# Leaky step of the two graph layers split between ScalarE and VectorE, and a new order of the work, in a four-layer graph kernel

## The chip, the cores and the metric

The kernel runs on one core of a Trainium2 chip. The metric is device time in microseconds for one execution over the whole batch; lower is better. The kernel before was run three times: 1826.78, 1825.92 and 1824.29 us, median 1825.92 us.

## What is computed

Four attention layers follow each other on 128 graphs of 128 nodes with 256 features, float32. Layers 0 and 2 are eight-head attention weighted by an adjacency matrix; layers 1 and 3 are single-head graph attention with a leaky step. The reference, cut:

```python
# layer 0 (_L0_gnn_ref): heads of 32, adj as a log weight, then out projection and layer norm
logits = jnp.einsum('bhqd,bhkd->bhqk', q, k) / np.sqrt(DK)
logits = logits + jnp.log(jnp.clip(adj, ADJ_MIN, None))[:, None, :, :]
attn = jax.nn.softmax(logits, axis=-1)
...
# layers 1 and 3 (_L1_gnn_ref, _L3_gnn_ref)
feat_proj = jnp.einsum('bnh,oh->bno', feats, fc_w) + fc_b
logits = q + jnp.swapaxes(k, 2, 1)                     # q, k: one column each from feat_proj
masked = logits + (1.0 - adj_mat) * NEG_INF
masked = jnp.where(masked >= 0, masked, LEAKY_SLOPE * masked)   # slope 0.01
atten = jax.nn.softmax(masked, axis=-1)
out = jnp.einsum('bnm,bmh->bnh', atten, feat_proj) + feats
...
# layer 2 (_L2_gnn_ref): heads of 32, a per-node bias pair, adj as a log weight, residual
```

## The kernel before, in words

The batch is cut into 64 groups of two graphs (GROUP = 2). The kernel is a software pipeline over turns: in turn t, each engine walks its own list in the table ORDER, and an entry (lag, name, where, n) means "do this step for group t - lag". So one turn does each step once, but for groups of different age: layer 0 for group t, layer 1 for t - 1, layer 2 for t - 2, layer 3 for t - 3 and so on. There are five lists, one for each engine, written out by hand; within an engine, nothing overtakes. The engines meet through semaphores only. Before the full turns the pipeline fills, after them it drains.

The steps the texts below speak of, by engine, with the lines of the profile:

- TensorE, the three-pass products (L877, L878, L879, function three_pass): each float32 product is made of three passes over split operands. q, k, v0 (layer 0) and q2, k2 take 12 matmuls each; each half of v2 (128x258), fc (128x258) and out_proj takes 6.
- TensorE, scores: 16 matmuls with 32-row weights (L942), once as "scores" and once, with sides exchanged, as "again"; between the two VectorE finds the row maximum. "A" is layer 0, "B" layer 2. B also adds column terms (L951), and "shift" (L965) subtracts the maximum. These go to banks 0 to 3 of PSUM.
- TensorE, sums: den (L986) and use (L977), 16 matmuls each with 32-column weights; wide (L992) spreads the inverse denominators.
- TensorE, transposes: turn_x (L1053), turn_max (L1047), turn_rows (L1098), mask (L1081, spreads the k column of a graph layer), turn_p (L1087, the softmaxed matrix). mix (L1093) is the last product of a graph layer.
- VectorE: max (L768) reads the four score banks in four reductions, all of which wait for the one semaphore of the last scores matmul; weigh (L792); den (L799, L801, L803); mask (L732 twice, then the leaky step L736 and its row minimum L739); inv (L855).
- ScalarE: soft (L547 and L551, exponentials of the scores), exp (L629) and inv (L636) of the graph layers, copies out of PSUM (among them turn_p, L641).

The leaky step works on negated logits, so that it is a minimum: min(x, 0.01 x). Before the change it is one VectorE instruction on a 128x256 tile in SBUF:

```python
dve.scalar_tensor_tensor(logits[layer][:, :, :], logits[layer][:, :, :], SLOPE,
                         logits[layer][:, :, :], ALU.mult, ALU.min).then_inc(leaked[layer], 1)
```

Steps other than scores take the banks 4 to 7 of PSUM in rotation, in the order of TensorE's list (BANK); wait_drained makes TensorE wait until the last user of a bank has been read (last_reader). FILLERS puts a few spare matmuls (L1031) ahead of some steps of the first groups.

## Time and profile before

| | |
|---|---|
| median of three runs | 1825.92 us |
| the profiled execution | 1827.11 us, span of the instructions 1825.2 us |
| PE busy | 1786.8 us (98% of the span) |
| DVE busy | 1496.7 us (82%) |
| ACT busy | 1345.0 us (74%) |
| POOL busy | 562.3 us (31%) |
| mean granted TensorE clock | 0.989 |

PE is TensorE's matmul row, PEld its weight loads, DVE VectorE, ACT ScalarE, POOL GpSimd. In the timeline a row gives the start, the duration and the instruction. Matmuls are pipelined, so their durations overlap; what a step takes of TensorE's time is the distance from its start to the start of the next step. A wait in brackets names what ended the engine's idle time.

### The profile page before, as it was taken

How to read it: one execution, taken by the hardware profiler on the slowest of the kernel's cores; microseconds unless marked ns; L12 is line 12 of the kernel's file. 1: busy time of each engine (PE TensorE's matmuls, PEld its weight loads, DVE VectorE, ACT ScalarE, POOL GpSimd, SP SyncE). 2: the span in 40 equal slices, each digit the busy share in tenths (PEclk: the TensorE clock that was granted, in tenths of full speed). 3: DMA queues.
4: the chain of work that ended last, by engine and by line, in shares of the span. 5: the costliest groups of instructions: out<-in, count | busy, mean ns of one | idle time of the engine just before them, and what ended most of it. 6: DMA issues, size and time to landing. Idle time of an engine off the chain costs nothing.

```text
span 1825.2 us, 69034 instructions
## 1 busy us (share of the span) xinstructions
PE 1786.8 (98%) x28449; PEld 1676.6 (92%) x28449; DVE 1496.7 (82%) x3359; ACT 1345.0 (74%) x3664; POOL 562.3 (31%) x667
## 2 busy tenths in 40 slices
PE   6999999999999999999999999999999999999996
PEld 6899999999999999999999999999999999999985
DVE  4678888888888888888888888888888888888885
ACT  3577787787787787787787787787787787787774
POOL 2232332332332332332332332332332332332321
PEclk7999999999999999999999999999999999999998
DMA  3111111111111111111111111111111111111100
GB/s 110 34 31 40 46 36 40 46 37 40 46 37 40 46 37 40 46 36 40 46 37 40 46 37 40 46 37 40 46 37 40 46 37 40 45 37 40 40 14 18
DMA packets 48260, 74.57 MB, mean 41 GB/s; under 512 B 5456, under 2 KB 21968, under 8 KB 47952
## 3 DMA queue, kind: packets, MB, share of 16 engines
q1 hardware_dynamic: 47376, 69.49, 12.1%
q8 instruction: 230, 3.77, 0.9%
q10 hardware_dynamic: 576, 0.68, 0.1%
q14 instruction: 78, 0.64, 0.1%
HBM read 53.37 MB, written 16.78 MB: 38 GB/s over the span
## 4 chain that ended last, share of the span: by engine, by line
PE 95%; DVE 3%; ACT 1%; issue 1%; POOL 0%; DVEq 0%; POOLq 0%; ACTq 0%
PE banks L877 17%; PE banks L942 15%; PE banks L879 15%; PE banks L878 15%; PE banks L986 7%; PE banks L1093 7%; PE banks L977 6%; PE banks L965 3%; PE banks L992 3%; PE banks L1081 2%; PE banks L1087 1%; PE banks L1053 1%; PE banks L1047 1%; PE banks L951 1%; PE banks L1031 0%
## 5 line engine op out<-in xcount | busy, mean ns | idle before, releaser
L478 POOL TENSOR_TENSOR weights_B<-weights_B,adj 128x512 f32<-128x512 f32 x64 | 82.4, 1288 | 815.9 <-ACT weights_B L551 815.9
L792 DVE TENSOR_TENSOR weights_A<-banks,adj 128x512 f32<-128x512 f32 x192 | 131.1, 684 | 77.2 <-ACT banks L547 77.1
L456 POOL TENSOR_TENSOR xt_lo<-x_t,xt_hi 128x512 fp32r<-128x512 f32 x64 | 82.1, 1282 | 335.6 <-ACT xt_hi L580 335.6
L877 PE MATMUL banks<-w_hi_f,xt_hi 128*128 128x258 f32 x512 | 164.6, 321 | 0.6 <-DVE xt_lo L656 0.6
L768 DVE TENSOR_REDUCE least_B<-banks 128x4 f32<-128x512 f32 x256 | 162.8, 678 | 0.0
L877 PE MATMUL banks<-w_hi_v,xt_hi 128*128 128x258 f32 (+1 forms) x512 | 152.2, 297 | 10.5 <-DVE w_lo_v L656 9.8
L768 DVE TENSOR_REDUCE least_cols_A<-banks 128x4 f32<-128x512 f32 x256 | 158.4, 681 | 4.5 <-PE banks L942 4.5
L636 ACT ACTIVATE logits<-logits,f_inv 128x128 f32<-128x128 f32 x256 | 90.9, 415 | 86.8 <-DVE f_inv L855 86.7
L877 PE MATMUL banks<-xt_hi,w_hi_q 128*128 128x256 f32 x512 | 150.5, 294 | 0.0
L879 PE MATMUL banks<-w_lo_v,xt_hi 128*128 128x258 f32 (+1 forms) x512 | 146.5, 286 | 0.0
L878 PE MATMUL banks<-w_hi_f,xt_lo 128*128 128x258 f32 x512 | 145.8, 285 | 0.0
L551 ACT ACTIVATE banks<-banks,v_B 128x256 f32<-128x256 f32 x384 | 145.5, 470 | 0.0
L878 PE MATMUL banks<-w_hi_v,xt_lo 128*128 128x258 f32 (+1 forms) x512 | 145.2, 284 | 0.0
L879 PE MATMUL banks<-xt_lo,w_hi_q 128*128 128x256 f32 x512 | 145.1, 283 | 0.0
L879 PE MATMUL banks<-w_lo_f,xt_hi 128*128 128x258 f32 x512 | 144.8, 283 | 0.0
L879 PE MATMUL banks<-xt_lo,w_hi_k 128*128 128x256 f32 x512 | 144.1, 281 | 0.0
L877 PE MATMUL banks<-xt_hi,w_hi_k 128*128 128x256 f32 x512 | 143.9, 281 | 0.0
L878 PE MATMUL banks<-xt_hi,w_lo_k 128*128 128x256 f32 x512 | 143.8, 281 | 0.0
L1093 PE MATMUL banks<-fpt,fp 128*128 128x128 f32 x1024 | 142.5, 282 | 1.3 <-DVE sum_t L816 0.7
L878 PE MATMUL banks<-xt_hi,w_lo_q 128*128 128x256 f32 x512 | 143.4, 280 | 0.0
L1093 PEld LDWEIGHTS banks<-fpt,fp 128*128 128x128 f32 x1024 | 125.2, 192 | 10.4 <-DVE sum_t L816 1.0
L792 DVE TENSOR_TENSOR weights_B<-banks,adj 128x512 f32<-128x512 f32 x192 | 128.2, 673 | 4.8 <-ACT banks L551 4.8
(185 smaller groups left out, 6068.5 us busy)
## 6 DMA issues: line engine op xcount, KB each, us to landing
x_t<-x_t_dram SPq DMA_DIRECT2D x64, 256.0 KB, 2.7
x_in<-x_dram SPq DMA_DIRECT2D x64, 256.0 KB, 2.6
out_dram<-x_out SPq DMA_DIRECT2D x64, 256.0 KB, 2.0
adj_t<-adj_t_dram SPq DMA_DIRECT2D x64, 128.0 KB, 2.1
adj<-adj_dram SPq DMA_DIRECT2D x64, 128.0 KB, 2.6
scratch<-weights_dram SPq DMA_DIRECT2D x9, 256.0 KB, 6.6
scratch<-weights_dram ACTq DMA_DIRECT2D x2, 256.0 KB, 4.8
out_bias<-L_gnn_bo_dram ACTq DMA_DIRECT2D x1, 128.0 KB, 7.5
```

Source lines behind the costliest of these rows:

```text
L478: pool.tensor_tensor(units, units, weight_of[where][:, G.four, :, :].unsqueeze(2).broadcast_to([P, GROUP, 2, P]), ALU.mult).then_inc(first ...
L551: last = act.activation(to[:, cols(g, 2 * P)], x[:, cols(g, 2 * P)], ACT.Exp, bias=v["B"][:, G.odd, g, DIM + 1:WIDE], scale=-1.0)
L636: last = act.activation(logits[where][:, g, :], logits[where][:, g, :], ACT.Copy, scale=f_inv[where][:, g:g + 1])
L768: dve.tensor_reduce(to, bank[SCORE_BANKS[n]].rearrange("p (u m) -> p u m", u=UNITS), axis=AX.X, op=ALU.min).then_inc(maxed[where], 1)
L792: dve.tensor_tensor(weights[where][:, n, :].rearrange(units, g=GROUP, h=2), bank[SCORE_BANKS[n]].rearrange(units, g=GROUP, h=2), weight_of ...
L877: pe.matmul(out_ap, left_hi(k), right_hi(k), start=(k == 0), stop=False)
L878: pe.matmul(out_ap, left_lo(k), right_hi(k), start=False, stop=False)
L879: last = pe.matmul(out_ap, left_hi(k), right_lo(k), start=False, stop=(k == KT - 1))
L942: last = pe.matmul(bank[SCORE_BANKS[r]][:, cols(u)], left[row_group(r), G.odd, half, cols(g)], right[row_group(r), G.odd, half, cols(g)], ...
L977: last = pe.matmul(to[row_group(r), cols(u)], v[s][:, G.odd, g, head:head + HEAD_DIM], weights[s][:, r, cols(u)], start=True, stop=True)
L986: last = pe.matmul(to[row_group(r), 0:P], sums[:, u, :], weights[s][:, r, cols(u)], start=(u == 0), stop=(u == UNITS - 1), skip_group_chec ...
L1093: last = pe.matmul(to[:, cols(k * GROUP + g)], fp[layer][:, g, cols(k)], fpt[layer][:, g, :], start=True, stop=True)
```

## The change

Two things are changed. First, the leaky step is split: ScalarE writes the copy scaled by 0.01 into the PSUM bank that the mask transposes had filled (it has been read by then), raises the new semaphore sloped, and VectorE takes the minimum of that copy and the logits. TensorE may use that bank again only when the minimum is done (leaked instead of masked). "leak" becomes a step of its own on both engines. Second, all five lists of ORDER are written anew; of these the diff below shows a line of each side.

```diff
--- before.py
+++ after.py
@@ -25,37 +25,38 @@
 ORDER = {
     "tensor": [
-        (0, "again", "A", 0), (0, "shift", "A", 0), (1, "fc", "1", 0), (2, "turn_rows", "2", 0), (3, "wide", "B", 0),
...
+        (0, "shift", "A", 0), (3, "wide", "B", 0), (1, "fc", "1", 0), (1, "fc", "1", 1), (2, "q", "2", 0),
...
@@ -266,6 +267,7 @@
         fp_ready = {n: sem(f"fp_ready_{n}") for n in "13"}
         qk_ready = {n: sem(f"qk_ready_{n}") for n in "13"}
         masked = {n: sem(f"masked_{n}") for n in "13"}
+        sloped = {n: sem(f"sloped_{n}") for n in "13"}
         leaked = {n: sem(f"leaked_{n}") for n in "13"}
         f_maxed = {n: sem(f"f_maxed_{n}") for n in "13"}
         f_exped = {n: sem(f"f_exped_{n}") for n in "13"}
@@ -344,7 +346,7 @@
             if name == "out_proj":
                 return summed, GROUP * g + n + 1
             if name == "mask":
-                return masked[where], GROUP * (g + 1)
+                return leaked[where], g + 1
             if name == "mix":
                 return (x2_ready if where == "1" else out_ready), g + 1
             return {"turn_x": x_biased.get(where), "turn_p": fpt_ready.get(where),
@@ -623,6 +625,11 @@
                     elif name == "fc":
                         act.wait_ge(filled[b], turn.after(G, *key))
                         act.activation(fp[where][:, n, :], bank[b][:, 0:WIDE], ACT.Copy).then_inc(fp_ready[where], 1)
+                    elif name == "leak":
+                        act.wait_ge(masked[where], GROUP * (G.no + 1))
+                        act.activation(bank[BANK["mask", where, 0]][:, 0:GROUP * P],
+                                       logits[where][:, :, :].rearrange("p g m -> p (g m)"), ACT.Copy, scale=SLOPE
+                                       ).then_inc(sloped[where], 1)
                     elif name == "exp":
                         act.wait_ge(f_maxed[where], G.no + 1)
                         for g in range(GROUP):
@@ -732,9 +739,14 @@
                     dve.scalar_tensor_tensor(logits[layer][:, g, :], bank[b][:, cols(g)],
                                              fp[layer][:, g, DIM:DIM + 1], penalty[:, G.four, g, :],
                                              ALU.add, ALU.add).then_inc(masked[layer], 1)
+
+            def leak(layer, G):
+
+                flat = logits[layer][:, :, :].rearrange("p g m -> p (g m)")
                 dve.wait_ge(masked[layer], GROUP * (G.no + 1))
-                dve.scalar_tensor_tensor(logits[layer][:, :, :], logits[layer][:, :, :], SLOPE,
-                                         logits[layer][:, :, :], ALU.mult, ALU.min).then_inc(leaked[layer], 1)
+                dve.wait_ge(sloped[layer], G.no + 1)
+                dve.tensor_tensor(flat, bank[BANK["mask", layer, 0]][:, 0:GROUP * P], flat, ALU.min
+                                  ).then_inc(leaked[layer], 1)
                 dve.wait_ge(leaked[layer], G.no + 1)
                 dve.tensor_reduce(f_neg_max[layer][:, :], logits[layer][:, :, :], axis=AX.X, op=ALU.min
                                   ).then_inc(f_maxed[layer], 1)
@@ -861,6 +873,8 @@
                                           ).then_inc(qk_ready[where], 1)
                     elif name == "mask":
                         mask(where, G, turn)
+                    elif name == "leak":
+                        leak(where, G)
                     elif name == "mix":
                         residual(where, G, turn)
 
```

Where the lists move work, in full turns:

TensorE, layer 0, from the scores of the next group to its maximum transposed (kt_A, qt_A: scores; least_cols_A: turn_max). Before:

```order
L1081 MATMUL banks<-ident,fp 128x128 x2
L942 MATMUL banks<-kt_A,qt_A 128x128 x16
L877 MATMUL banks<-w_hi_v,xt_hi 128x258
L878 MATMUL banks<-w_hi_v,xt_lo 128x258
L879 MATMUL banks<-w_lo_v,xt_hi 128x258
L877 MATMUL banks<-w_hi_v,xt_hi 128x258
L878 MATMUL banks<-w_hi_v,xt_lo 128x258
L879 MATMUL banks<-w_lo_v,xt_hi 128x258
L1053 MATMUL banks<-ident,x 128x128 x4
L986 MATMUL banks<-weights_B,sums 32x128 x16
L977 MATMUL banks<-weights_B,v_B 32x128 x16
L1047 MATMUL banks<-ident,least_cols_A 128x128
```

After:

```order
L893 MATMUL banks<-xt_lo,w_hi_k 128x256
L956 MATMUL banks<-kt_A,qt_A 128x128 x16
L991 MATMUL banks<-weights_B,v_B 32x128 x16
L1000 MATMUL banks<-weights_B,sums 32x128 x16
L1112 MATMUL banks<-ident,c_cols 128x128
L1067 MATMUL banks<-ident,x 128x128 x4
L1061 MATMUL banks<-ident,least_cols_A 128x128
L956 MATMUL banks<-qt_A,kt_A 128x128 x16
L979 MATMUL banks<-least_rows_A,minus_pick 128x128 x16
```

Behind the scores stood one half of v2, the x transposes, den B and use B; now use B, den B, turn_rows and the x transposes stand there, the half of v2 has gone ahead of mask 3, and the second scores pass and its shift follow.

TensorE, layer 2, from its scores on (kt_B, qt_B: scores). Before:

```order
L986 MATMUL banks<-weights_A,sums 32x128 x16
L977 MATMUL banks<-weights_A,v_A 32x128 x16
L942 MATMUL banks<-kt_B,qt_B 128x128 x16
L951 MATMUL banks<-c_rows,minus_pick 128x256 x8
L1093 MATMUL banks<-fpt,fp 128x128 x4
L877 MATMUL banks<-xt_hi,w_hi_q 128x256
```

After:

```order
L956 MATMUL banks<-kt_B,qt_B 128x128 x16
L965 MATMUL banks<-c_rows,minus_pick 128x256 x8
L1000 MATMUL banks<-weights_A,sums 32x128 x16
L991 MATMUL banks<-weights_A,v_A 32x128 x16
L1101 MATMUL banks<-ident,logits 128x128 x2
L891 MATMUL banks<-xt_hi,w_hi_q 128x256
```

Where mix 3 (fpt, fp) followed the column terms (c_rows), den A and use A now follow them, and the transposes of layer 1's matrix (logits) come next.

VectorE, layer 1, around the mask (fp, penalty). Before:

```order
L792 TENSOR_TENSOR weights_A<-banks,adj 128x512
L816 TENSOR_TENSOR sum_t<-banks,sum_t 128x512
L860 TENSOR_TENSOR fp<-fp,cols_tile 128x2x2
L792 TENSOR_TENSOR weights_A<-banks,adj 128x512
L732 SCALAR_TENSOR_TENSOR logits<-banks,fp,penalty 128x128 x2
L736 SCALAR_TENSOR_TENSOR logits<-logits 128x256
L739 TENSOR_REDUCE f_neg_max<-logits 128x2
L799 RECIPROCAL banks<-banks 128x128
L801 CAST inv_hi_A<-banks 128x128
L803 SCALAR_TENSOR_TENSOR inv_parts_A<-banks,low_row,inv_hi_A 128x128
L656 TENSOR_TENSOR xt_lo<-sum_t,xt_hi 128x512
```

After:

```order
L804 TENSOR_TENSOR weights_A<-banks,adj 128x512
L872 TENSOR_TENSOR fp<-fp,cols_tile 128x2x2
L804 TENSOR_TENSOR weights_A<-banks,adj 128x512
L739 SCALAR_TENSOR_TENSOR logits<-banks,fp,penalty 128x128 x2
L804 TENSOR_TENSOR weights_A<-banks,adj 128x512
L748 TENSOR_TENSOR logits<-banks,logits 128x256
L751 TENSOR_REDUCE f_neg_max<-logits 128x2
L797 TENSOR_SCALAR adj<-adj_t 128x256
L780 TENSOR_REDUCE least_B<-banks 128x4
L867 RECIPROCAL f_inv<-f_den 128x2
L780 TENSOR_REDUCE least_B<-banks 128x4
```

The mask and the leaky step were neighbours; now the third weighting of A lies between them, and a copy of adj and the first maximum of B between the row minimum and the reciprocal f_inv.

## Rows read from the trace of the kernel before

**Rows 1.** Windows view, full turns: busy us of each engine, then granted clock

```profile
800.00:1200.00 400.00, 400.00 (x6480) 376.54 (x6479) 338.14 (x762) 305.63 (x835) 128.42 (x148) 1.00 0.13 40
```

**Rows 2.** Waits from 200 to 1600 us: TensorE's longest entry (total, times, longest)

```profile
PEld banks L942 <- issue: 27.4, 153, 0.2
```

**Rows 3.** Timeline of PE, one full turn: start us, duration us, instruction

```profile
805.93 0.28 PE L877 MATMUL banks<-w_hi_v,xt_hi 128*128 128x258 f32 x1
806.65 0.28 PE L877 MATMUL banks<-xt_hi,w_hi_k 128*128 128x256 f32 x1
808.09 0.38 PE L1081 MATMUL banks<-ident,fp 128*128 128x128 f32 x2
808.40 1.17 PE L942 MATMUL banks<-kt_A,qt_A 32*128 32x128 f32 x32
809.50 0.39 PE L877 MATMUL banks<-w_hi_v,xt_hi 128*128 128x258 f32 x1
810.33 0.60 PE L1053 MATMUL banks<-ident,x 128*128 128x128 f32 x4
...
811.75 1.06 PE L977 MATMUL banks<-weights_B,v_B 128*32 128x128 f32 x32
812.74 0.33 PE L1047 MATMUL banks<-ident,least_cols_A 128*128 128x128 f32 x1
813.00 1.17 PE L942 MATMUL banks<-qt_A,kt_A 32*128 32x128 f32 x32
813.91 0.66 PE L965 MATMUL banks<-least_rows_A,minus_pick 4*128 4x128 f32 x16
...
822.80 0.50 PE L951 MATMUL banks<-c_rows,minus_pick 2*128 2x256 f32 x8
823.23 1.16 PE L1093 MATMUL banks<-fpt,fp 128*128 128x128 f32 x8
...
825.63 0.38 PE L1087 MATMUL banks<-ident,logits 128*128 128x128 f32 x2
825.77 0.37 PE L877 MATMUL banks<-w_hi_f,xt_hi 128*128 128x258 f32 x1
826.59 0.56 PE L992 MATMUL banks<-inv_parts_A,spread 128*128 128x128 f32 x4
826.98 0.33 PE L877 MATMUL banks<-w_hi_f,xt_hi 128*128 128x258 f32 x1
827.76 1.05 PE L1093 MATMUL banks<-fpt,fp 128*128 128x128 f32 x8
...
837.71 0.60 PE L1053 MATMUL banks<-ident,x 128*128 128x128 f32 x4
```

**Rows 4.** Timeline of PE while the pipeline fills: layer 0 scores and their maximum

```profile
49.61 1.17 PE L942 MATMUL banks<-kt_A,qt_A 32*128 32x128 f32 x32 [0.98 <-issue]
...
53.38 0.33 PE L1047 MATMUL banks<-ident,least_cols_A 128*128 128x128 f32 x1 [0.19 <-DVE least_cols_A L768]
```

**Rows 5.** Chain view, 50 to 54 us: the four reductions between the two

```profile
50.84 2.50 DVE least_cols_A L768 x4
```

**Rows 6.** Timeline of PE: three-pass product (the last 12) and the scores behind it

```profile
70.67 0.28 PE L877 MATMUL banks<-xt_hi,w_hi_k 128*128 128x256 f32 x1
...
72.20 1.06 PE L942 MATMUL banks<-kt_A,qt_A 32*128 32x128 f32 x28
```

**Rows 7.** Timeline of DVE and ACT, full turn: mask, leaky step, a 128x256 copy

```profile
808.58 0.61 DVE L732 SCALAR_TENSOR_TENSOR logits<-banks,fp,penalty 128x128 f32<-128x128 f32 x2 [0.51 <-PE banks L1081]
809.22 0.42 DVE L736 SCALAR_TENSOR_TENSOR logits<-logits 128x256 f32<-128x256 f32 x1
...
826.57 0.39 ACT L641 ACTIVATE fpt<-banks 128x256 f32<-128x256 f32 x1
```

**Rows 8.** Timeline of PE in the drain: mask 3, then turn_p 3, group 63

```profile
1814.53 0.40 PE L1081 MATMUL banks<-ident,fp 128*128 128x128 f32 x2 [0.77 <-DVE fp L860]
1818.55 0.66 PE L1087 MATMUL banks<-ident,logits 128*128 128x128 f32 x2 [3.62 <-ACT logits L636]
```

18 lines of the change are left out of this document (13 added, 5 removed), and 35 rows, old and new, of the table ORDER.

## The prediction

> **What bounds the kernel now.** I read the windows first. In the full turns TensorE is busy 400.00 of 400 us at the full granted clock, VectorE 338 and ScalarE 306 [rows 1]. Then the waits: from 200 to 1600 us the longest entry of TensorE is one of weight loads, 27.4 us over 153 times, released by nothing but issue; the matmul row itself has none [rows 2]. So a full turn costs what TensorE's own list costs, step after step. From one turn_x to the next, 810.33 to 837.71, that is 27.38 us [rows 3]. 64 turns of it are 1752 of the span of 1825; the rest is fill and drain. Of the 64, about 60 have all four layers at work. 0.2% of the time, 3.65 us, is what a measurement of this kernel can tell from no change: 0.06 us per full turn decide the sign.
>
> **The split itself.** It takes one VectorE instruction of 0.42 us out and puts another over the same 128x256 elements in; I cost the exchange at 0. ScalarE gains one 128x256 instruction, 0.39 us by the copy of that size [rows 7], 128 times: 50 us more on an engine with about 94 us idle in 400 [rows 1]. No engine that bounds anything gets less to do. What the split costs is latency: behind the mask stand now a ScalarE instruction and two handoffs, at 0.03 us each (VectorE's next instruction on its own result starts 0.03 us after the mask's end, 808.58 + 0.61 to 809.22 [rows 7]). So 0.45 us more from mask to turn_p. The bank that is held until the minimum is done costs nothing in full turns: the next user of the mask 1 bank is turn_p 1, which waits for that chain anyway; that of the mask 3 bank is turn_rows, with k2 (1.4), scores A, use B and den B ahead of it.
>
> **The new order, outside the scores of A.** TensorE's list does the same matmuls; what differs is which step follows which. The prices of those seams are in the timeline. Six three-pass matmuls in mid-run take 0.72 us (805.93 to 806.65), twelve 1.44 (806.65 to 808.09); after scores six take 0.83, after transposes 0.82 (825.77 to 826.59), after wide 0.78. Two transposes ahead of scores take 0.31; ahead of three-pass work 0.24, which is 0.14 (825.63 to 825.77) plus the 0.10 by which the six behind them are late [rows 3]. So one transpose is 0.12, and 0.07 more stand ahead of scores; I take the same 0.07 ahead of den. Hence, per turn:
> - the half of v2 no longer stands behind scores A: -0.11;
> - the second half of fc 3 no longer stands behind wide: -0.06;
> - turn_p 3 stands ahead of wide A and not of den A: -0.07;
> - turn_rows goes to the stretch at the scores of A, which is priced below: -0.12;
> - mask 3 ahead of k2 and not of scores: -0.07;
> - v0 ahead of scores B, k2 ahead of scores A: twelve matmuls ahead of scores took 1.53 (70.67 to 72.20 [rows 6]) and not 1.44, so +0.09 twice, +0.18;
> - use A ahead of transposes and not of scores: one transpose ahead of scores would be 0.19 by these prices and took 0.26 behind use (812.74 to 813.00), +0.07.
> The work behind shift and behind mix changes partners within the same kind, and one set of transposes stands ahead of wide in either list: 0. Sum: -0.18 us.
>
> One seam is not in the trace: den A directly behind the column terms of scores B. Behind them mix came after 0.43 us (822.80 to 823.23 [rows 3]), with nothing to see of a price. The dearest neighbour is the 0.11 of three-pass work behind scores. Between 0 and 0.11, I take 0.05: mix is the same kind of neighbour of the very same step, but den uses other weight shapes.
>
> **The new order, at the scores of A.** Before, scores A to turn_max A took 808.40 to 812.74, 4.34 us, 0.83 of it the half of v2: 3.51 without it [rows 3]. In the new list use B, den B, turn_rows and the x transposes fill the stretch: x transposes, den B and use B took 2.41 (810.33 to 812.74), turn_rows is 0.12, and scores themselves, 0.91 (813.00 to 813.91) to 1.10 (808.40 to 809.50), make it 3.44 to 3.63 us. But turn_max A must wait for four reductions, and these for the last scores matmul. Where VectorE was free, the whole took 49.61 to 53.38, 3.77 us, TensorE waiting at its end [rows 4], with 2.50 us of reductions in it [rows 5]. VectorE is free there in the new list: mask 3 starts 0.49 us behind its transposes, which stand 1.74 us ahead of scores A, and mask, ScalarE's copy, minimum and row minimum need 0.61 + 0.45 + 0.42 + 0.42, so they are done 0.65 us behind the start of scores, ahead of the 1.23 (49.61 to 50.84) at which the reductions can start. So TensorE now waits here every turn, and the stretch costs 3.77 whatever its steps cost: +0.26 us per turn against 3.51. What is late next is the low half of x behind those reductions and den B: it ends about 5.9 us behind the start of scores, fc 1 can start at about 6.05. Hidden by little.
>
> The Trainium skill (TensorEngine Tiling (Array Packing), Key Properties) says that changing the tiling mode drains TensorE. The trace agrees in kind: scores with 32-row weights cost 1.10 ahead of three-pass work, 0.91 ahead of the shift, which keeps to few rows as well. Counted by that rule alone the new list has 10 changes of mode per turn and the old one 11, and the order would be a small gain. The sum above doesn't use the rule; the wait on the reductions is what it leaves out.
>
> **Fill, drain and the sum.** In the fill the k products of group 1 move ahead of out_proj; the 0.98 us that TensorE stood still ahead of the next scores [rows 4] should go, and I take -0.9 us and no more, since turn_x of group 0 still follows the layer norm. In the drain the leaky chain of group 63 is on the path: mask 3 to turn_p 3 took 1814.53 to 1818.55, 4.02 us, with TensorE idle [rows 8], and becomes 4.47; and den B, which the path goes through, now stands behind use B, +0.99 by the same row of use (811.75 to 812.74). Together +0.5. Full turns: -0.18 + 0.05 + 0.26 = +0.13 us, 60 times, +7.8. Sum +8.3: 1827.1 becomes 1835.4 for the profiled execution, which lies 1.2 above the median of the three; from the median I forecast **1834.2 us**.
>
> **The rivals.**
> - *Faster by mode changes.* If the new neighbours cost nothing (0.18 for v0 and k2 ahead of scores, 0.07 for use A ahead of transposes, and den A behind the column terms 0 and not 0.05), the turn outside the stretch at A loses 0.18 + 0.25 = 0.43, against the 0.26: -0.17, times 60, -10.2 us, with +0.5 at the ends 1816.2. It decides from 0.32 us saved outside the stretch. For it: runs of three-pass work are longer now, with two fewer starts of such a run split off by wide. Against: the price ahead of scores is there to see [rows 6]. That is also where the skill's rule points. Chance 0.18.
> - *No change.* Seams and the wait cancel, the turn stays within 0.06 us: 1822.3 to 1829.6. It needs errors of 0.1 in my seams, each rounded to 0.01 but several taken from a neighbour. Chance 0.22.
> - *The leaky chain stalls TensorE.* In the new list v0, scores B, column terms, den A and use A lie between mask 1 and turn_p 1: 1.53 + 0.1 + 0.91 + 0.43 + 1.86 (den and use, 2.41 less the four transposes ahead of them, 4 x 0.12 + 0.07) and the mask's own 0.14, about 5.0 us. The chain alone needs 4.47 (4.02 [rows 8] and the 0.45), and it must pass VectorE's third weighting of A and first maximum of B and ScalarE's scaling of layer 3. Two of these are about a quarter of the four reductions' 2.50 us each [rows 5], the third a little more, 1.9 us together, and they fall partly into the chain's own gaps. If 0.8 of it is in the way, turn_p 1 is late by 0.27: +0.40 per turn, +24 us, 1850. It decides from a delay of 0.5 us. Chance 0.15.
> - *The split doesn't do what its form suggests*, relieve VectorE: 0.42 us may stay 0.42. It has no price of its own here, as VectorE doesn't bind, and no chance beside the others.
>
> **How the numbers follow.** The forecast case, +0.06 to +0.30 per turn, 1829.6 to 1844.5, has 0.45. Faster 0.18, same 0.22, slower 0.45 + 0.15 = 0.60. Range: below, half of the faster case, 1821; above, half of the stall, 1847. The ends' unknowns (each ±1.5 us) are inside.
>
> **What would show it.** In the profile after: a TensorE wait at turn_max A on the reductions of A, 0.1 to 0.4 us in every turn, some 60 entries (right); none, and the turn shorter (the stretch is wrong). The turn by two turn_x starts: 27.51 expected; 27.2 speaks for the mode changes. A wait of TensorE at turn_p 1 on ScalarE's scaling would be the third rival. VectorE's minimum at 0.42 us; ScalarE's copy near 0.39. Scores B to den A: 0.43 for the column terms if the unseen seam is free. The last mask 3 to turn_p 3 near 4.5 us. A granted clock below 1.0 in full turns would make all of it wrong.

## The result, and the profile after

The changed kernel takes **1860.39 us**, median of 4 runs (1858.63 to 1861.72), against 1825.43 of the kernel before (1824.29 to 1826.78, 4 runs): a ratio of 1.0189, 95% interval 1.0176 to 1.0202. It is slower by 35.0 us, where 8.3 were forecast. The profiled execution has a span of 1859.8 us (before 1825.2).

The busy times of the page first, then the windows that answer to [rows 1] and the waits that answer to [rows 2]; the last line is the row of turn_max before, which [rows 2] does not show.

```profile
PE 1805.9 (97%) x28449; PEld 1686.2 (91%) x28449; DVE 1529.5 (82%) x3359; ACT 1405.3 (76%) x3792; POOL 562.9 (30%) x667
```

```profile
800.00:1200.00 400.00, 397.99 (x6416) 372.36 (x6414) 342.96 (x752) 314.62 (x853) 125.77 (x145) 1.00 0.13 40
```

```profile
PEld banks L956 <- issue: 18.5, 100, 0.2
PEld banks L1061 <- issue: 16.3, 50, 0.3
PEld banks L1095 <- issue: 7.8, 47, 0.2
```

```profile
PEld banks L1047 <- issue: 10.1, 51, 0.2
```

Three things are to be seen. The clock is full in the full turns in both kernels, so what a turn costs more is not clock. TensorE is busy 397.99 of 400 and its matmul rows have no wait at all between 200 and 1600 us, as before. And in the weight loads' rows one entry has grown: L1061, the transposes of turn_max, 16.3 us over 50 times, where it was 10.1 over 51 before (L1047), and the mask's (L1095) is new. The ends of matmuls are modelled, so a short stop lies under the tail of the matmul before it; it is read from one start to the next.

This is the stretch from the scores of A to turn_max A in a full turn, TensorE's timeline, and with it VectorE's (start, duration, instruction):

```profile
848.39 1.17 PE L956 MATMUL banks<-kt_A,qt_A 32*128 32x128 f32 x32
849.49 1.08 PE L991 MATMUL banks<-weights_B,v_B 128*32 128x128 f32 x32
850.39 1.06 PE L1000 MATMUL banks<-weights_B,sums 128*32 128x128 f32 x32
851.38 0.33 PE L1112 MATMUL banks<-ident,c_cols 128*128 128x128 f32 x1
851.54 0.60 PE L1067 MATMUL banks<-ident,x 128*128 128x128 f32 x4
852.26 0.30 PE L1061 MATMUL banks<-ident,least_cols_A 128*128 128x128 f32 x1
```

```profile
849.63 2.48 DVE L780 TENSOR_REDUCE least_cols_A<-banks 128x4 f32<-128x512 f32 x4 [0.40 <-PE banks L956]
```

The reductions start 0.14 us behind the start of use B, which follows the last scores matmul, and end at 852.11; turn_max A starts at 852.26. That distance of 0.15 us is the same, to 0.001, in all full turns, which is what a step looks like that starts as soon as it is released; before the change it was 0.25 in the median and 0.15 at the least, so the old order was near this wait too. The four x transposes ahead of it take 0.72 us from start to start, where they take 0.44 if nothing waits (e4 and e6 below). Scores A to turn_max A is 3.87 us.

By the starts of scores A, the 58 turns from the sixth to the last take 27.705 us each (155.84 to 1762.72); before they took 27.381 (151.44 to 1739.52). That gives the account of the 34.6 us between the two spans:

| | before | after | more |
|---|---|---|---|
| to the sixth scores A | 151.4 | 155.8 | 4.4 |
| 58 full turns | 1588.1 | 1606.9 | 18.8 |
| last scores A to the end | 85.7 | 97.1 | 11.4 |

### The profile page after: what moved, and what is told of

Its sections match the earlier page's. It is cut to its first block, busy times and chain, and to the rows that moved or that the text cites. A ratio compares the mean times of both kernels' runs of the same rounds, so it can differ in the third digit from the quotient of the medians.

```text
span 1859.8 us, 69291 instructions
## 1 busy us (share of the span) xinstructions
PE 1805.9 (97%) x28449; PEld 1686.2 (91%) x28449; DVE 1529.5 (82%) x3359; ACT 1405.3 (76%) x3792; POOL 562.9 (30%) x667
## 3 DMA queue, kind: packets, MB, share of 16 engines
q8 instruction: 230, 3.77, 0.9%
## 4 chain that ended last, share of the span: by engine, by line
PE 95%; DVE 2%; issue 1%; ACT 1%; DMA 0%; SPq 0%; POOL 0%; DVEq 0%; POOLq 0%
PE banks L891 16%; PE banks L956 15%; PE banks L893 15%; PE banks L892 15%; PE banks L1107 7%; PE banks L991 6%; PE banks L1000 6%; PE banks L1006 3%; PE banks L979 3%; PE banks L1095 2%; PE banks L1101 2%; PE banks L1067 1%; PE banks L1061 1%; PE banks L965 1%; PE banks L1112 1%
## 5 line engine op out<-in xcount | busy, mean ns | idle before, releaser
L780 DVE TENSOR_REDUCE least_B<-banks 128x4 f32<-128x512 f32 x256 | 168.0, 681 | 39.2 <-PE banks L965 39.2
L891 PE MATMUL banks<-xt_hi,w_hi_k 128*128 128x256 f32 x512 | 155.5, 304 | 0.0
L891 PE MATMUL banks<-w_hi_f,xt_hi 128*128 128x258 f32 x512 | 151.8, 296 | 0.1
L553 ACT ACTIVATE banks<-banks,v_B 128x256 f32<-128x256 f32 x384 | 151.4, 467 | 0.0
L811 DVE RECIPROCAL banks<-banks 128x128 f32<-128x128 f32 x128 | 122.4, 956 | 7.2 <-PE banks L1000 7.2
```

Of the source, the lines that this page charges most:

```text
L553: last = act.activation(to[:, cols(g, 2 * P)], x[:, cols(g, 2 * P)], ACT.Exp, bias=v["B"][:, G.odd, g, DIM + 1:WIDE], scale=-1.0)
L780: dve.tensor_reduce(to, bank[SCORE_BANKS[n]].rearrange("p (u m) -> p u m", u=UNITS), axis=AX.X, op=ALU.min).then_inc(maxed[where], 1)
L811: dve.reciprocal(bank[b][:, 0:P], bank[b][:, 0:P]).then_inc(inverted[where], 1)
L891: pe.matmul(out_ap, left_hi(k), right_hi(k), start=(k == 0), stop=False)
```

## The experiments

Fourteen kernels. "Turn" is always taken as above, from the sixth scores A to the last; "drain" is from the last scores A to the end of the span.

**e1: the split alone, in the old order.**

```diff
@@ before: scalar list @@
-        ... (5, "turn_p", "3", 0), (4, "turn_x", "3", 0), ...
+        ... (5, "turn_p", "3", 0), (2, "leak", "1", 0), (4, "turn_x", "3", 0), ...
-        (2, "k", "2", 0), (1, "norm", "", 0), ...
+        (2, "k", "2", 0), (4, "leak", "3", 0), (1, "norm", "", 0), ...
```

> The old order with the split alone: ScalarE's scaled copy stands right behind the mask on its list (ahead of norm in layer 3, behind turn_p 3 in layer 1). If the order makes the loss, TensorE stays without waits in full turns, a turn stays at 27.38 us, and the only price is the copy and its handoffs in the last leaky chain, 0.5 to 1 us: 1826 to 1827. If the split itself delays TensorE (its latency, or the ScalarE time ahead of norm), the turn is longer by 0.05 us or more and the time is above 1829.

Measured: 1857.28 us, ratio 1.0173 (1.0156 to 1.0190); turn 27.854, drain 89.1. The split isn't free in the old order. ScalarE's copy for layer 3 stands ahead of the layer norm and waits for the mask; the norm's last instruction ends at 820.02 and TensorE waits for it at the x transposes:

```profile
820.16 0.63 PE L1061 MATMUL banks<-ident,x 128*128 128x128 f32 x4 [0.28 <-ACT x L558]
```

```profile
818.62 0.39 ACT L629 ACTIVATE banks<-logits 128x256 f32<-128x256 f32 x1
818.94 1.08 ACT L558 ACTIVATE x<-x,less,rstd 128x256 f32<-128x256 f32 x2
```

**e2: the new order alone, without the split** (VectorE's old one-instruction leaky step in the place of the minimum, no copy on ScalarE).

```diff
-                dve.wait_ge(sloped[layer], G.no + 1)
-                dve.tensor_tensor(flat, bank[BANK["mask", layer, 0]][:, 0:GROUP * P], flat, ALU.min
-                                  ).then_inc(leaked[layer], 1)
+                dve.scalar_tensor_tensor(flat, flat, SLOPE, flat, ALU.mult, ALU.min).then_inc(leaked[layer], 1)
```

> The new order with the old one-instruction leaky step at the same place of VectorE's list. If the order makes the loss, this is 1857 to 1861, a turn of 27.7 us. If the split makes it, it is below 1840, a turn below 27.5.

Measured: 1857.79 us, 1.0174 (1.0159 to 1.0189); turn 27.701, drain 95.7. The turn is that of the changed kernel to 0.004 us: in the new order the split costs nothing in full turns, and their loss is the order's.

**e3: GpSimd's list moved**, so that its penalty and adjacency steps are not beside VectorE's bias add ahead of mask 1.

```diff
-        (1, "penalty", "", 0), (0, "adj_t", "", 0), (0, "bias", "0", 0), (3, "weigh", "B", 0), (4, "bias", "3", 0),
-        (1, "rstd", "", 0), (-1, "turn_x", "0", 0), (0, "weigh", "A", 0)],
+        (3, "weigh", "B", 0), (4, "bias", "3", 0), (1, "rstd", "", 0), (0, "adj_t", "", 0), (0, "penalty", "", 0),
+        (-1, "turn_x", "0", 0), (0, "bias", "0", 0), (0, "weigh", "A", 0)],
```

> The changed kernel; GpSimd's penalty, bias 0 and adj steps are moved away from the place where VectorE adds the biases of layer 1 (L872, 128x4, which lasts 0.61 us beside a GpSimd step and 0.16 in layer 3). Theory 1, TensorE waits on VectorE's string of work from the maximum of A to the third weighting of A: that instruction falls to 0.16, TensorE waits less at mask 1 and ahead of scores B, and the turn falls from 27.71 to 27.45 to 27.55. Theory 2, the new neighbours on TensorE cost more than I took: the turn stays at 27.71.

Measured: 1849.78 us, 1.0132 (1.0116 to 1.0147); turn 27.543, 0.16 less than the changed kernel. In the changed kernel VectorE's add over 128x4 elements takes as long as GpSimd's step beside it, and mask 1 waits for it; the timelines of VectorE, GpSimd and TensorE:

```profile
856.81 0.61 DVE L872 TENSOR_TENSOR fp<-fp,cols_tile 128x4 f32<-128x4 f32 x1
```

```profile
856.79 0.61 POOL L474 TENSOR_TENSOR penalty<-penalty,big 128x256 f32<-128x256 f32 x1
```

```profile
857.57 0.40 PE L1095 MATMUL banks<-ident,fp 128*128 128x128 f32 x2
```

The slow add is not new. Before the change it took 0.55 us beside another GpSimd step (VectorE's and TensorE's timeline of before), but mask 1 started 0.66 us behind its end; in the changed kernel it starts 0.15 behind it in 44 of 47 full turns between 300 and 1600 us, in e3 0.45.

```profile
818.26 0.55 DVE L860 TENSOR_TENSOR fp<-fp,cols_tile 128x4 f32<-128x4 f32 x1
819.47 0.38 PE L1081 MATMUL banks<-ident,fp 128*128 128x128 f32 x2
```

In e3 the same add stands alone and takes 0.15 (VectorE's timeline), 0.158 in the mean of its 102, where the changed kernel has 0.371 (both layers together, VectorE's groups between 200 and 1600 us, e3's first):

```profile
824.57 0.15 DVE L872 TENSOR_TENSOR fp<-fp,cols_tile 128x4 f32<-128x4 f32 x1
```

```profile
L872 DVE TENSOR_TENSOR fp<-fp,cols_tile 128x4 f32<-128x4 f32 x102 | 16.1, 158 | 0.0
```

```profile
L872 DVE TENSOR_TENSOR fp<-fp,cols_tile 128x4 f32<-128x4 f32 x101 | 37.4, 371 | 0.0
```

The q2 products ahead of mask 1 take 1.58 us from start to start in the changed kernel and 1.43 in e3.

**e4 and e6: the row maximum of A over 32 of 128 columns**, so that VectorE's four reductions end earlier; e6 with GpSimd's list of e3 as well. The other 96 columns are left out of the maximum of A.

```diff
-                        dve.tensor_reduce(to, bank[SCORE_BANKS[n]].rearrange("p (u m) -> p u m", u=UNITS),
+                        part = P if where == "B" else P // 4
+                        dve.tensor_reduce(to, bank[SCORE_BANKS[n]].rearrange("p (u m) -> p u m", u=UNITS)[:, :, 0:part],
```

> The changed kernel with the four reductions of A over a quarter of the columns: the row maximum of layer 0 is taken over 32 of 128 columns of each head only. Theory 1, with the wait on the reductions at turn_max A and the string behind them: scores A to turn_max A falls from 3.87 to about 3.7, the waits at mask 1 and scores B go, the turn is 27.2 to 27.4. Theory 2: the turn stays above 27.6, since TensorE's own neighbours set it.

> The changed kernel with both waits of TensorE taken away at once: the row maximum of layer 0 over 32 of 128 columns only, and GpSimd's steps moved as in e3. If the two waits add up and nothing else is in the way, the turn is 27.20 to 27.28: that is what the order of TensorE's steps costs by itself, and below the 27.38 of before. If it stays at 27.40 there is a third wait behind them.

Measured, one run each: e4 1837.57, turn 27.406; e6 1827.50, turn 27.228. So 0.30 us per turn hang on the reductions (27.705 to 27.406), 0.16 on the bias add, and both together are gone in e6 (0.48, against 0.46 as the sum). By the starts, e4's gain lies at the x transposes (0.72 to 0.44) and at turn_max A (0.23 to 0.20) and nowhere else by more than 0.01, so it is not that VectorE had less to do everywhere. In e6 the row of waits at turn_max is missing from the weight loads. The new order without its two waits is 0.15 us per turn faster than the old one.

**e5: the split in the old order, fitted**, with ScalarE's copy behind the norm and VectorE's minimum behind the reductions of A; exp and inv of layer 3 move back with them.

```diff
@@ e1: vector list @@
-        ... (-1, "max", "A", 3), (0, "turn_x", "1", 0),
+        ... (-1, "max", "A", 3), (3, "leak", "3", 0), (0, "turn_x", "1", 0),
@@ e1: scalar list @@
-        (2, "k", "2", 0), (4, "leak", "3", 0), (1, "norm", "", 0), (2, "v", "2", 1), (1, "turn_x", "1", 0), ...
+        (2, "k", "2", 0), (1, "norm", "", 0), (2, "v", "2", 1), (4, "leak", "3", 0), (1, "turn_x", "1", 0), ...
```

> The old order with the split, but its steps where there is room: in layer 3 ScalarE's copy behind norm and the second half of v2, VectorE's minimum behind the four reductions of A, exp ahead of the exponentials of A. If e1 lost its 0.47 us per turn only because the copy stood ahead of norm, for which the x transposes wait, the turn is back at 27.38 to 27.45 and the time 1826 to 1832: the split costs nothing in itself. If the split has no place in the old order, the turn stays above 27.6 and the time above 1842.

Measured: 1900.60 us, 1.0406 (1.0389 to 1.0424), turn 28.550: a miss. The mask's bank is now held until the minimum is done, and in the old list's rotation of four banks the bank of mask 3 is that of use B. TensorE's waits between 200 and 1600 us:

```profile
PE banks L989 <- DVE logits L746: 28.1, 49, 0.6
```

By the starts use B comes 0.76 us later behind den B than before, of the 1.17 that the turn is longer; the rest stands at fc 1 and v0, and no run places it.

**e7 and e10: k2 moved under the wait**, between the x transposes and turn_max A, with e3's GpSimd list and ScalarE's list laid out to fit; e7 also puts VectorE's third weighting of A ahead of mask 1, e10 den B ahead of use B.

```diff
@@ e3: tensor list, e7 @@
-        ... (3, "mask", "3", 0), (1, "k", "2", 0), (-1, "scores", "A", 0),
-        (2, "use", "B", 0), (2, "den", "B", 0), (1, "turn_rows", "2", 0), (0, "turn_x", "1", 0),
+        ... (3, "mask", "3", 0), (-1, "scores", "A", 0),
+        (2, "use", "B", 0), (2, "den", "B", 0), (1, "turn_rows", "2", 0), (0, "turn_x", "1", 0), (1, "k", "2", 0),
@@ e10 @@
+        (2, "den", "B", 0), (2, "use", "B", 0), (1, "turn_rows", "2", 0), (0, "turn_x", "1", 0), (1, "k", "2", 0),
```

> The changed kernel, nothing left out: k2 (1.4 us of TensorE) is moved in between the scores of A and turn_max A, so that TensorE has work while VectorE reduces; GpSimd's steps as in e3; the third weighting of A ahead of mask 1 on VectorE. If the wait on the reductions was what cost 0.28 us per turn, the turn falls to 27.2 to 27.35 and the time, with the fill and drain of the changed kernel, to 1828 to 1838. If the turn stays at 27.5 or more, the work moved has only changed which wait ends last.

> The changed kernel with GpSimd's list as in e3, and the k products of layer 2 moved between the x transposes and the turn of the row maxima of A, as in e7; but den B ahead of use B, so that the rotation gives turn_max A the bank of use B (drained by ScalarE early) and not that of den B (held by VectorE until the split of the inverse). Theory (what cost 0.3 us per turn is TensorE waiting for the four reductions of A; e7 failed on the bank alone): with 1.44 us of work under them the wait goes, full turn 27.23 as in e6, fill and drain as in e3 (the whole about 1831). Rival (mask 3 directly ahead of scores A puts the leaky chain of layer 3 in front of the reductions on VectorE, so that they end later by about 1 us, and TensorE waits in spite of k2): full turn 27.5 to 27.7, the whole 1847 to 1858. Second rival (another bank now holds, as turn_x behind mask 3's bank): over 28.

Measured: e7 1936.36 us, 1.0608 (1.0592 to 1.0624), turn 29.01; e10 2052.09, 1.1248 (1.1221 to 1.1274), turn 31.02. Banks are given out in the list's order, one of four after another, so a fill that is moved shifts those of all between. In e7 turn_max A got the bank of den B, in e10 k2 did, and VectorE holds that bank until it has split the inverse; without k2 ahead of it scores A also comes before VectorE's last weighting of B. The waits, e7 and then e10:

```profile
PE banks L1061 <- DVE inv_parts_B L815: 32.4, 48, 0.7
PE banks L956 <- DVE weights_B L804: 16.9, 48, 0.6
```

```profile
PE banks L891 <- DVE inv_parts_B L815: 95.4, 45, 2.1
PE banks L1095 <- DVE fp L872: 22.4, 42, 0.5
PE banks L956 <- DVE weights_B L804: 16.0, 45, 0.6
```

**e8, e9, e11: steps moved in the drain.** mix 3 and fc 3 of groups 61 and 62 go ahead of turn_max B of the group behind them, with their copies. e8 has den B ahead of use B besides; e11 is e10 with e9's moves.

```diff
+MOVES = {
+    "tensor": [(key, g - (key[0] == "mix"), ("turn_max", "B", 0), g + 1) for g in (LAST - 2, LAST - 1)
+               for key in (("mix", "3", 0), ("fc", "3", 0), ("fc", "3", 1))],
...
+}
@@ e8 besides @@
-        (2, "use", "B", 0), (2, "den", "B", 0), (1, "turn_rows", "2", 0), (0, "turn_x", "1", 0),
+        (2, "den", "B", 0), (2, "use", "B", 0), (1, "turn_rows", "2", 0), (0, "turn_x", "1", 0),
```

> The changed kernel; in the last turns alone mix 3 and fc 3 of groups 61 and 62 go ahead of turn_max B of the next group, as in the old order, with the turn_x 3 steps that feed them; and den B ahead of use B in all turns. If the drain is longer by 11 us because these steps stand between the shift of B and the sums of B, it falls from 97 us (scores of A of group 63 to the end) to 88 to 93 and the time to 1852 to 1857. If it stays at 96 to 98, the drain is set by something else. The full turn should stay at 27.7.

> The changed kernel, its full turns untouched; only in the last turns the residual product and the two fc products of layer 3 of groups 61 and 62 stand ahead of TensorE's turn of the row maxima of B of the next group, and their x transposes' copies ahead on ScalarE and VectorE. (The run before this one that moved them also put the denominator of B ahead of its use, and that stalled every turn.) Theory (in the drain these thirty matmuls stand between the shift of B and the use of B of the following group, on the path, at half clock, while TensorE waits for the leaky chain ahead of turn_max B anyway): full turn 27.70 as in the changed kernel, the drain from the last scores A 91 instead of 97.1 us, the whole about 1854. Rival (the drain is bound by the leaky chain and by the number of steps that follow one another, whatever stands between): drain 96 to 97, the whole 1860. Second rival: moved ahead, they delay the scores B chain of the last groups by as much as they free: within 1 us of 97.

> The kernel of e10 with the moves in the drain of e9. Theory (turn and drain are costs of their own and add up): turn as in e10, drain as in e9, the whole that of e10 less what e9 gains over the changed kernel, about 6 us; with both theories right 1825, no slower than the kernel before. Rival (the moves help only where the leaky chain is late, and k2 between takes that room): the gain of e9 is halved, the whole 3 us over the sum.

Measured: e8 2028.38 us, 1.1107 (1.1090 to 1.1124), turn 30.44, drain 95.7, again with turn_max A in the bank of den B. e9 1861.49, 1.0189 (1.0173 to 1.0204), turn 27.678, drain 97.2: the drain doesn't shorten, the rival was right. e11 2058.38, 1.1273 (1.1254 to 1.1292), not told apart from e10. In e8:

```profile
PE banks L1081 <- DVE inv_parts_B L835: 74.2, 46, 1.6
```

Where the drain's time is, the windows tell: the last scores A to scores B of group 61, on to 62, to 63, and to the end. Columns: stretch, us; busy us of PE, PEld, DVE, ACT, POOL with instructions; granted clock; DMA. Before and after:

```profile
1739.52:1752.12 12.60, 12.50 (x253) 11.08 (x252) 11.04 (x24) 10.74 (x31) 3.92 (x4) 1.00 0.01 3
1752.12:1774.01 21.89, 19.25 (x267) 17.33 (x263) 17.33 (x42) 15.21 (x45) 3.19 (x4) 1.00 0.04 14
1774.01:1791.93 17.92, 14.94 (x228) 13.44 (x228) 13.10 (x28) 12.43 (x38) 2.29 (x2) 1.00 0.05 16
1791.93:1825.20 33.27, 18.39 (x213) 15.21 (x213) 14.90 (x31) 10.60 (x31) 3.30 (x3) 0.73 0.07 24
```

```profile
1762.72:1773.75 11.03, 9.46 (x181) 8.36 (x181) 10.03 (x21) 9.21 (x25) 2.47 (x3) 1.00 0.01 2
1773.75:1799.03 25.28, 22.49 (x327) 20.54 (x327) 18.81 (x44) 16.48 (x46) 3.17 (x4) 0.93 0.04 13
1799.03:1821.67 22.64, 17.75 (x228) 16.22 (x228) 12.95 (x28) 13.13 (x40) 2.27 (x2) 0.85 0.04 13
1821.67:1859.80 38.13, 22.32 (x215) 19.10 (x215) 14.78 (x31) 12.02 (x35) 3.31 (x3) 0.63 0.06 21
```

All of the 4.9 us by which the last stretch grew stand between again B and wide B of group 63, 9.43 us before and 14.41 after: mix 3 and fc 3 of the group ahead stand in it now, and the granted clock is 0.59 there. The windows of that piece, before and after:

```profile
1797.27:1806.70 9.43, 5.80 (x115) 4.70 (x115) 5.35 (x12) 4.21 (x14) 2.26 (x2) 0.66 0.01 3
1826.56:1840.97 14.41, 11.08 (x135) 10.08 (x135) 6.42 (x14) 6.33 (x19) 2.27 (x2) 0.59 0.05 20
```

Over the whole drain instructions are about as many (961 matmul records before, 951 after), but TensorE is busy 72.0 us with them instead of 65.1, at a lower granted clock in each of the last three stretches, and idle 25.1 instead of 20.6: +6.9 and +4.5 of the 11.4. e9, busy 68.5 us in its drain, wins 3.5 of the busy time back and loses it as idle time (28.7). It takes the piece from again B to wide B down to 11.65 us, and the pieces ahead of it grow by as much.

**e12, e13: the second half of v2 moved under the wait**, which k2 was not fit for; turn_rows, which needs its columns, behind again A and in the same bank; ScalarE's list follows, and GpSimd's is e3's. e13 with its banks laid by hand.

```diff
@@ e3: tensor list @@
-        (1, "v", "2", 0), (1, "v", "2", 1), (3, "mask", "3", 0), (1, "k", "2", 0), (-1, "scores", "A", 0),
-        (2, "use", "B", 0), (2, "den", "B", 0), (1, "turn_rows", "2", 0), (0, "turn_x", "1", 0),
-        (-1, "turn_max", "A", 0), (-1, "again", "A", 0)],
+        (1, "v", "2", 0), (3, "mask", "3", 0), (1, "k", "2", 0), (-1, "scores", "A", 0),
+        (2, "use", "B", 0), (2, "den", "B", 0), (0, "turn_x", "1", 0), (1, "v", "2", 1),
+        (-1, "turn_max", "A", 0), (-1, "again", "A", 0), (1, "turn_rows", "2", 0)],
@@ e13 @@
+BANK.update({("k", "2", 0): 7, ("use", "B", 0): 6, ("turn_x", "1", 0): 7, ("v", "2", 1): 5, ("turn_rows", "2", 0): 5,
+             ("turn_max", "A", 0): 6})
```

> The changed kernel with GpSimd's list as in e3, and on TensorE the second half of v2 (six matmuls, 0.72 us) between the x transposes and the turn of the row maxima of A; turn_rows, which needs its columns, goes behind again A; ScalarE's list follows; the bank of turn_rows is set to that of v2's second half. k2 stays ahead of scores A (in e7 and e10 its move brought scores A ahead of VectorE's last weighting of B and put two fills into a bank that VectorE held). Theory (the reductions of A end 3.62 to 3.72 us behind the start of scores A, and TensorE has 3.44 to 3.6 us of work there; 0.72 more covers them, and in the table of banks no fill now follows one that is held): full turn 27.24 plus or minus 0.06, which is e6's turn with all 128 columns reduced; fill and drain as in e3, the whole 1832 plus or minus 2. Rival (the wait at the reductions was not what cost 0.3 us, e4 and e6 gained because VectorE had less to do everywhere): turn 27.5, the whole 1847. Second rival (a bank holds again, this time turn_x behind the leaky chain of mask 3): over 27.7, with a row TensorE turn_x waits for VectorE's logits in the waits.

> The kernel of e12 with its banks laid out by hand, since in e12 turn_x stood in the bank that fc 1 fills next, and fc 1 waited 1.0 us per turn for ScalarE's bias copy out of it: turn_x back behind k2 in bank 7 (next fill q2), use B and turn_max A in 6, v2's second half and turn_rows in 5. Theory (TensorE's wait at turn_max A on the reductions, which e12 no longer shows, scores A to turn_max A being 4.21 us with 0.81 of v2 in it, is what cost 0.3 us per turn): full turn 27.24 plus or minus 0.08, the whole 1832 plus or minus 3. Rival (the wait is only moved: scores A comes 0.7 us earlier in the turn, and something else, the bias copy or the low half of x, is then late by that): turn 27.5 or more, with a row of waits for it.

Measured: e12 2031.83 us, 1.1138 (1.1115 to 1.1161), turn 30.43; e13 1875.55, 1.0277 (1.0262 to 1.0293), turn 27.972. In e12 the x transposes stand in the bank that fc 1 fills next, and fc 1 waits for ScalarE's bias copy out of it. Behind that pause of 1.0 us the granted clock falls, so the turn pays twice: the matmul that waited, and the windows behind it.

```profile
813.62 0.39 PE L892 MATMUL banks<-w_hi_f,xt_hi 128*128 128x258 f32 x1 [1.02 <-ACT xb_t L593]
```

```profile
812.00:814.00 2.00, 0.98 (x9) 0.84 (x8) 1.26 (x2) 1.94 (x4) 1.20 (x1) 1.00 0.71 194
814.00:816.00 2.00, 2.00 (x13) 2.00 (x12) 0.82 (x2) 0.44 (x2) 0.07 (x1) 0.53 0.02 7
816.00:818.00 2.00, 2.00 (x13) 2.00 (x12) 0.86 (x2) 1.36 (x3) 0.00 (x0) 0.61 0.00 0
```

In e13 the banks are right and the wait at the reductions is gone. TensorE's timeline of the same stretch, and VectorE's reductions in it, which end at 803.23, ahead of the turn_max at 803.72:

```profile
802.50 0.66 PE L1069 MATMUL banks<-ident,x 128*128 128x128 f32 x4
...
803.72 0.27 PE L1063 MATMUL banks<-ident,least_cols_A 128*128 128x128 f32 x1
803.92 1.17 PE L958 MATMUL banks<-qt_A,kt_A 32*128 32x128 f32 x32
805.16 0.30 PE L1114 MATMUL banks<-ident,c_cols 128*128 128x128 f32 x1
```

```profile
800.75 2.48 DVE L782 TENSOR_REDUCE least_cols_A<-banks 128x4 f32<-128x512 f32 x4
```

The x transposes take 0.41 us instead of 0.72: 0.31 won. But the turn got 0.43 longer than e3's. Both halves of v2 together now take 0.93 + 0.81 = 1.74 us instead of 1.44 (0.30 lost), again A takes 1.24 instead of 0.92 because turn_rows behind it waits for ScalarE's copy of its columns (0.32 lost), and turn_rows takes 0.23 instead of 0.16. That is 0.38 of the 0.43; most of the rest is mask 3, 0.18 instead of 0.14. Of the 0.30 about 0.09 is the second half's new place (0.81 instead of 0.72). The other 0.21 is a wait of the same kind as at mask 1: only half of v2 is left between fc 3 and mask 3, and mask 3 now starts 0.15 us behind the end of VectorE's bias add of layer 3 in every full turn, where it had 0.67 in e3 (VectorE's and TensorE's timeline):

```profile
797.45 0.16 DVE L874 TENSOR_TENSOR fp<-fp,cols_tile 128x4 f32<-128x4 f32 x1
797.76 0.40 PE L1097 MATMUL banks<-ident,fp 128*128 128x128 f32 x2
```

The move pays for what it hides. So e13 shows the wait and its size, and misses the turn it was to give.

**e14: e13 with the v products of layer 0 in another bank than the q products that follow them at the start.**

```diff
-BANK.update({("k", "2", 0): 7, ...
+BANK.update({("v", "0", 0): 6, ("k", "2", 0): 7, ...
```

> The kernel of e13, and the v products of layer 0 in bank 6 instead of 5, so that q0, which follows v0 directly in the first turn, has not the bank that ScalarE is still to copy v0 from. Theory (the start is late because q0 waits for ScalarE's copy of v0, which stands behind eight copies of weights): scores A of the first group at 18.1 us instead of 20.6, the next ones earlier by up to that, full turn unchanged, the whole 1 to 3 us less than e13. Rival (the start is late by the arrival of the weights or by the low clock that follows anyway): scores A still at 20 or later, the whole as e13. Second rival (den A, which now follows v0 in bank 6, waits for its copy in full turns): the turn longer by 0.2 or more.

Measured: 1874.77 us, 1.0266 (1.0249 to 1.0283), turn 27.962. The first scores A comes at 17.98 instead of 20.51, as the theory said; by the third group it stands at 73.79 against 73.93, and the whole is e13's within the spread of either. In the changed kernel q0 starts 0.09 us behind ScalarE's copy of v0 (ScalarE's and TensorE's timeline; the row names another releaser, which had been done):

```profile
13.13 0.58 ACT L613 ACTIVATE v_A<-banks 128x512 f32<-128x512 f32 x1
```

```profile
13.80 0.55 PE L891 MATMUL banks<-xt_hi,w_hi_q 128*128 128x256 f32 x1 [1.05 <-DVE w_lo_k L663]
```

No kernel here beat the one before. e6 came to 1827.50, with most of a maximum left out.

## Why the prediction was wrong

The direction and the forecast wait on the reductions of A were right; the size was off fourfold, and 1860.4 lies outside the range of 1821 to 1847. The full turns came to +18.8 us where +7.8 were summed, fill and drain to +15.8 where "Together +0.5" stood, so both sums failed, and the ends by more. Step by step:

- **The split costs nothing on VectorE and 0.39 on ScalarE, off the path: right in the new order.** VectorE's minimum takes 0.425 us in the mean, as the old instruction did, ScalarE's copy 0.389. The turn with and without the split is 27.705 and 27.701 (e2). The bank that is held did no harm there; it did in the old order (e5), which the prediction did not look at.
- **The mask-to-turn_p chain, 4.47 at the end: right.** 1848.63 to 1853.14 is 4.51 us, answering to [rows 8]:

```profile
1848.63 0.40 PE L1095 MATMUL banks<-ident,fp 128*128 128x128 f32 x2 [0.77 <-DVE fp L872]
1853.14 0.66 PE L1101 MATMUL banks<-ident,logits 128*128 128x128 f32 x2 [4.10 <-ACT logits L643]
```

- **The seams outside the stretch, -0.18 + 0.05: right in sign, too small.** Without its two waits the new turn is 0.15 shorter (e6), and its stretch at the scores of A, 3.59 us of TensorE's own work, is 0.08 longer than the 3.51 of before. So the seams elsewhere gave -0.23 where -0.13 was the sum. The unseen seam, den A behind the column terms, has no price: 0.42 us of column terms and then den, as with mix before [rows 3]. One seam that the sum left out is that of fc 1: its halves took 0.83 and 0.76 us in the old list, behind shift and behind wide, and 1.50 together in the new one, 0.10 less. The other terms are not taken apart here.
- **The stretch, 3.77: right in kind, short by 0.10.** It is 3.87. The reductions start 1.24 us behind the scores and take 2.48, as forecast; turn_max starts 0.15 behind their end, and in the row of the fill from which 3.77 was taken it was 0.04 [rows 4, 5]. 0.36 more than 3.51, where 0.26 was taken, is 6 us over 58 turns.
- **The failed step of the turn: "Full turns: -0.18 + 0.05 + 0.26 = +0.13 us".** A second wait is missing in it. In the old list v0 and q2, 2.9 us of work, lie between fc 1 and mask 1; in the new one q2 alone, 1.4, and mask 1 then waits for VectorE's bias add, which takes 0.61 us beside a GpSimd step (0.55 before, where v0 covered it). It is 0.16 per turn (e3), 9.5 us in all. The prediction took TensorE's move and GpSimd's list at nothing here, without naming what covered the add. With it: -0.23 + 0.36 + 0.16 = +0.29, against the +0.324 measured; the 0.03 left is turn_max A itself, 0.23 us to the start of again A while it waits and 0.20 in e6, which has no wait.
- **The failed step of the fill, "I take -0.9 us": +4.4 in the profiled execution.** The k products ahead of out_proj did bring scores A of the second group forward, 46.52 against 49.61, and the 0.98 us of [rows 4] went. But turn_x of the first group then waits 3.0 us for the norm, and in this execution the clock falls behind that. The profiled execution of e9, whose lists are the same up to the last turns, has no fall in the same window; its sixth scores A is at 152.08, 3.8 us earlier, against 151.44 before. e2's has no fall either (152.78), e3's has one (154.97). So the order costs the fill 0.6 to 1.3 us without the fall, and the rest goes with the fall, which comes in some executions only. Windows of the changed kernel and of e9:

```profile
50.00:55.00 5.00, 4.27 (x31) 4.00 (x35) 2.54 (x5) 1.99 (x5) 1.27 (x1) 0.50 0.01 3
```

```profile
50.00:55.00 5.00, 4.68 (x74) 4.25 (x72) 1.43 (x3) 2.79 (x6) 2.47 (x2) 1.00 0.02 5
```

- **The failed step of the drain, 0.45 + 0.99, so +1.4: it is +11.4.** Both terms taken are there: mask to turn_p at 4.51, and den B behind use B, which takes 1.68 us at the lower clock of the drain (1836.09 to 1837.77) and not the 0.99 of a full turn. But they were all that was looked at. Ahead of them the stretches between the last scores B are 3.4 and 4.7 us longer, as clock and as idle time, and the last stretch is 4.9 longer, with mix 3 and fc 3 now inside it; the first is 1.6 shorter. The new order without the split has 95.7 (e2), the old order with it 89.1 (e1), the one before 85.7: 10.0 us belong to the order and 1.4 to 3.4 to the split. The clock falls in the stretches in which TensorE idles more, which the windows suggest as cause; no run took the one without the other, and e9's try at the idle time failed, so how the 10.0 come about step by step stays open.
- **The rivals.** Faster by mode changes: the seams did give 0.23, short of the 0.32 that it wanted. The Trainium skill (TensorEngine Tiling (Array Packing), Key Properties) says that changing the tiling mode drains TensorE; the new list has one such change fewer per turn, and the runs don't part its share of the 0.23 from the neighbours' own. The leaky chain stalling turn_p 1: no wait there in full turns; it came only in the drain. Clock below 1.0 in full turns: no.

The sum by measured terms: 4.4 + 58 x 0.324 + 11.4 = 34.6, the difference of the spans.

## What to carry to other kernels

Where one engine is the bound and its list is laid out anew, go through every step that waits for another engine and ask what work lay between it and its source before, and what lies there now; do it for the engines that look idle too, since a small step of theirs may stand beside the one instruction that matters. Price the ends of the program as orders of their own: here 16 of 35 us were fill and drain, where each step moved is bare. The same add was harmless before, with 0.5 us to spare, and cost 0.16 us a turn once v0 no longer covered it. A table that gives out buffers by position is part of the order: of the eight kernels e5, e7, e8 and e10 to e14, six ran into a buffer that another engine held, with waits of 0.6 to 2.1 us per turn, so print the rotation before and after each move.

## What was not expected of the hardware

- **A VectorE instruction over 4 columns can last until the end of a GpSimd instruction that began before it.** The add over 128x4 took 0.15 us alone and 0.61 beside a 128x256 GpSimd step of 0.61: it ends at 857.42, GpSimd's at 857.40. Where the GpSimd step starts behind the add, as in layer 3 (845.92 behind 845.84), the add keeps its 0.16. The Trainium skill (SBUF — State Buffer, SBUF: two separate sides) says that VectorE, with two inputs in SBUF, and GpSimd take a shared pair of ports as a lock for the whole instruction, whichever of them starts first. The trace agrees in both cases, in the first to 0.02 us. The minimum, one of whose inputs the change moved to PSUM, is no faster in the mean for it, 0.425 against 0.425.
- **Waits that cost 1% don't show as idle time.** 0.30 us per turn at turn_max and 0.16 at mask 1 have no row in the matmul waits; the first has a weight-load row of 0.33 released by "issue", the second one of 0.17. Only the starts tell them, or a run without them: the waiting step stands 0.15 us behind the end of what it waits for, turn after turn.
- **A pause of TensorE may be paid again as clock, and may not.** In e12, 1.02 us of pause were followed by windows with a granted clock of 0.53 and 0.61, mostly the lower level of 1.2 GHz, where a matmul of 256 columns comes every 0.21 us instead of every 0.12; e13 has the same lists with other banks, and e12's turn is 2.5 us longer than its: 1.2 at the pause, the rest in fc 1 and q2 behind it. In e13 and the changed kernel, with pauses of at most about 0.3 per turn, it stays at 1.00. In e10, 2.1 us of pause per turn left the clock at 0.98 between 800 and 1200 us, where e12 has 0.94 and e8, with 1.6, 0.96. What else decides, the runs don't tell.
